# Relational message loop of a four-layer GNN: two pieces share one PSUM bank and one completion signal, sums run twelve pieces behind, sixteen weight slots

## The reference, cut to what matters

```
weight = einsum('rb,bio->rio', w_comp, bases)          # 32 relations, 8 bases
xw     = einsum('ni,rio->nro', h, weight)
msg    = xw[src, rel_type] * norm
out    = segment_sum(msg, dst, num_segments=6250)
x      = layernorm(x + relu(out))
```

## Time and profile before

| | |
|---|---|
| median of three executions | 7899.04 us |
| the profiled execution, device time | 7916.77 us |
| its span, first to last instruction | 7915.0 us |
| granted TensorE clock, mean over the span | 0.803 |
| layer 2's edge loop, first gather to last sum | 3486 to 5045 us |

### The profile page before, as it was taken

How to read it: one execution, slowest core, us unless ns; L and a number is a source line. 1 busy time by engine, 2 the same in 40 slices (tenths; PEclk the granted TensorE clock), 3 DMA queues, 4 the chain that set the end, 5 groups by cost and what they waited for, 6 DMA issues and landing times. The chain is left out here.

```text
span 7915.0 us, 120335 instructions
## 1 busy us (share of the span) xinstructions
PE 5430.0 (69%) x23622; PEld 3980.9 (50%) x23625; DVE 5308.3 (67%) x12633; ACT 2715.6 (34%) x10214; POOL 4371.6 (55%) x7065
## 2 busy tenths in 40 slices
PE   6265666634767676866666666799577777777798
PEld 4133333322444444335555555688455555555687
DVE  8677666676766675546666665774577777777666
ACT  1022222221322222224444444211455555565211
POOL 0377777726777776466666666100466666666311
PEclk8576676666777777877777777999788888888899
DMA  3132333323333333343343333355355555555411
GB/s 109 54 88 81 87 87 87 86 76 105 106 108 107 116 106 91 120 129 113 112 116 110 105 118 108 113 160 162 98 143 143 144 143 140 146 143 140 90 43 38
DMA packets 449612, 865.34 MB, mean 109 GB/s; under 512 B 78488, under 2 KB 284424, under 8 KB 448906
## 3 DMA queue, kind: packets, MB, share of 16 engines
q0 software_dynamic: 194048, 574.45, 26.3%
q1 hardware_dynamic: 238442, 251.25, 10.2%
q10 hardware_dynamic: 16416, 31.99, 1.2%
HBM read 718.55 MB, written 298.46 MB: 128 GB/s over the span
## 5 line engine op out<-in xcount | busy, mean ns | idle before, releaser
L860 PE MATMUL ps<-ring 128*128 x3528 | 1489.4, 547 | 1000.5 <-issue 304.9
L860 PEld LDWEIGHTS ps<-ring 128*128 128x128 f32 x3528 | 727.2, 252 | 1494.2 <-issue 1458.0
L1557 PE MATMUL ps<-big,ring 128*128 128x128 f32 x4928 | 959.8, 355 | 573.6 <-issue 246.6
L834 ACT CAST ring<-ohb 128x128 f32<-128x128 bf16 x1764 | 523.8, 298 | 2044.8 <-DVE ohb L797 1254.8
L1557 PEld LDWEIGHTS ps<-big,ring 128*128 128x128 f32 x4928 | 842.6, 253 | 682.0 <-issue 424.1
L761 POOL DMA_INDIRECT ring<-xl_d,idx x832 | 846.2, 1017 | 611.2 <-DVEq L580 263.5
L1481 POOL DMA_INDIRECT big<-x_d,idx x832 | 805.1, 968 | 572.8 <-ACT ring L1509 425.4
L1773 POOL DMA_INDIRECT ring<-kv_d,gidx x754 | 723.0, 959 | 609.0 <-issue 492.3
L761 POOL DMA_INDIRECT ring<-x_d,idx x832 | 835.3, 1004 | 314.2 <-issue 126.8
L797 DVE TENSOR_SCALAR ohb<-iotab,keyf,nbase 128x128 bf16<-128x128 bf16 x1764 | 588.8, 334 | 463.6 <-remote 174.0
L807 DVE TENSOR_TENSOR big<-big,ps 128x257 f32 (+1 forms) x1764 | 755.0, 428 | 209.8 <-issue 154.9
(11 more groups left out here) (428 smaller groups left out, 9885.8 us busy)
## 6 DMA issues: line engine op xcount, KB each, us to landing
bas_d<-big SPq DMA_DIRECT2D x1232, 128.0 KB
att_d<-wreg SPq DMA_DIRECT2D x464, 132.0 KB
big<-bas_d SPq DMA_DIRECT2D x49, 1024.0 KB, 5.6
x_d<-ring SPq DMA_DIRECT2D x147, 128.0 KB, 1.7
gh_d<-aside ACTq DMA_DIRECT2D x49, 384.0 KB
ring<-xl_d,idx POOLq DMA_INDIRECT x832
ring<-x_d,idx POOLq DMA_INDIRECT x832
big<-x_d,idx POOLq DMA_INDIRECT x832
```

Source lines behind the costliest of these rows:

```text
L834: S.copy(ohf[:, q % G1, :], ohb[:, q % G1, :]).then_inc(e["ohf"], 1)
L860: T.matmul(ps[k][:, 0:D], ohf[:, k, :], rows[:, slot, :].rearrange("p a d -> p (a d)"), start=True, stop=True)
L1557: last = nc.tensor.matmul(ps[c % BANKS2][:, 0:FW].rearrange("p (n h b) -> p n h b", n=NB, h=H)[:, :, h, :], xs[:, j, h * P:(h + 1) * P], w ...
```

## The change

Five things are changed, all in layer 2's edge loop. The weights get 16 slots in place of 8, and VectorE's wait before a group looks 16 pieces back. Two neighbouring pieces write the two halves (256 columns each) of one PSUM bank, so seven banks hold 14 pieces. TensorE signals `l2_mm` after the second piece of a pair, and all waits on `l2_mm` count pairs. It waits for a free bank only before the first piece of a pair. `L2_LAG` goes from 6 to 12. ScalarE's row slots (16), the gather slots (32), the eight running sums and the flush are as before.

```diff
-        wts = nodef[:, 0:8 * P].rearrange("p (s n b) -> p s n b", s=8, b=BASES)
+        wts = nodef[:, 0:16 * P].rearrange("p (s n b) -> p s n b", s=16, b=BASES)
...
                 if past(c, 16):
-                    act.wait_ge(l2_mm, c + GRP - 16)
+                    act.wait_ge(l2_mm, (c + GRP - 16) // 2)
...
-                    if past(c, 8):
-                        dve.wait_ge(l2_mm, c + GRP - 8)
+                    if past(c, 16):
+                        dve.wait_ge(l2_mm, (c + GRP - 16) // 2)
                     for a in range(GRP):
-                        V.scalar_tensor_tensor(out=wts[:, (j + a) % 8], in0=iota[:, 0:NB].unsqueeze(2).broadcast_to([P, NB, BASES]),
+                        V.scalar_tensor_tensor(out=wts[:, j + a], in0=iota[:, 0:NB].unsqueeze(2).broadcast_to([P, NB, BASES]),
...
-                    dve.wait_ge(l2_mm, cc + 1)
+                    dve.wait_ge(l2_mm, cc // 2 + 1)
...
-                                           in1=ps[cc % BANKS2][:, 0:FW], op0=ALU.mult, op1=ALU.add).then_inc(l2_cur, 1)
+                                           in1=ps[cc // 2 % BANKS2][:, cc % 2 * FW:(cc % 2 + 1) * FW], op0=ALU.mult, op1=ALU.add).then_inc(l2_cur, 1)
...
-        L2_LAG = 6
+        L2_LAG = 12
         BANKS2 = 7
...
-                if past(c, BANKS2):
-                    pe.wait_ge(l2_cur, c - BANKS2 + 1)
+                if c % 2 == 0 and past(c, 2 * BANKS2):
+                    pe.wait_ge(l2_cur, c - 2 * BANKS2 + 2)
+                bank = ps[c // 2 % BANKS2][:, c % 2 * FW:(c % 2 + 1) * FW]
                 for h in range(H):
-                    last = nc.tensor.matmul(ps[c % BANKS2][:, 0:FW].rearrange("p (n h b) -> p n h b", n=NB, h=H)[:, :, h, :],
-                                            xs[:, j, h * P:(h + 1) * P], wts[:, j % 8], start=True, stop=True)
-                last.then_inc(l2_mm, 1)
+                    last = nc.tensor.matmul(bank.rearrange("p (n h b) -> p n h b", n=NB, h=H)[:, :, h, :],
+                                            xs[:, j, h * P:(h + 1) * P], wts[:, j], start=True, stop=True)
+                if c % 2:
+                    last.then_inc(l2_mm, 1)
```

## The result

| | before | after |
|---|---|---|
| median, 12 executions each, same chip | 7901.31 us | 7886.35 us |
| ratio | | 0.9981 [0.9972, 0.999] |
| span of the profiled execution | 7915.0 us | 7898.1 us |
| edge loop, first gather to last sum | 1558.7 us | 1544.4 us |

The change takes 15 us off, at 0.19% just what this measurement can tell. Of the 16.9 us between the two profiled spans 14.3 lie in the edge loop; the loop starts 2.2 us earlier, and 0.4 us come behind it.

A forecast was written before the change was run, and what follows sets the result against it. The prediction took SP's flush queue in layer 2's edge loop as the bound. Less SP waiting (33 us) plus an earlier start (5 us) made 38 us off 7899, giving 7861 us, range 7790 to 7920.

The forecast's parts named there:

- the frame: Layer 2's edge loop: SP's flush queue is all but full and sets the pace; VectorE's waits for TensorE are not the bound.
- Rival A: Edge loop: flush queue no bound, VectorE's waits for TensorE are real time; shorter GpSimd gaps give 132 us, 7767 us; chance 0.13.
- Rival C: Edge loop: gathers without gaps leave SP no quick stretch; up to 41 us slower, 7940 us; 0.14 with any other loss.
- rival B: Edge loop: nothing gained, as sums are still signalled late during gathers; within 16 us of 7899; 0.28 with forecast's low end.
- the prediction's sign: Middle of the edge loop: if right, SP's waits for sums fall from 51 us to under 20.
- What VectorE gives SP is an end to SP's own waiting: at most the 51.3 us ... I take three quarters of them, 33 us: Edge loop's middle: VectorE's stock of pieces ends SP's waits for sums; 33 us off, bounds 0 and 51.
- The start, "5 us": Edge loop's start: about four more pieces pass early with the longer lag; 5 us off, bounds 0 and 10.
- The lag: Edge loop: with weight slots, twelve pieces in hand let VectorE work through nearly all of its 5.5 us hole.
- The zeros: Edge loop: one signal for two pieces, ScalarE's wait with GpSimd's gap, and bank halves each change the time by 0.
- The end: Edge loop's last 66 us: twelve sums in place of six follow the last weight; 0, at most 3 us lost.

The follow-up runs named there:

- g0: Kernel before with masked wait values and ScalarE waiting once per group of four pieces, slow instructions (fourth batch): 7928.61 us, 1.0018 against the kernel before.
- g1: Changed kernel with masked wait values and ScalarE waiting once per group of four pieces, slow instructions: 7908.12 us, 0.9995 against the kernel before.
- g2: Changed kernel with the single masked ScalarE wait and sums six pieces behind in place of twelve, slow instructions: 7904.56 us, 0.9995 against the kernel before.
- f0: Kernel before with ScalarE's single masked wait per group, in a batch with quick instructions: 0.9997 against the kernel before (6974.68 us).
- one-wait pair: Kernel before and changed kernel, each with ScalarE's single masked wait per group, slow instructions: 7928.61 us (1.0018) and 7908.12 us (0.9995).
- e5: Changed kernel with masked waits plus one unused semaphore increment per piece on the sync queue: 8022.25 us, 1.0138; masked base 1.0027.
- the fourth batch: Single masked ScalarE wait on the kernel before and the changed one, the latter also with lag six or twelve running sums; unmodified kernel before 7911.71 us.

## Why the prediction was right or wrong

The direction and the frame held. **The bound** is the flush queue: one more instruction costs 87 us, more ring gains nothing, the queue lacked a finished sum for only 28.8 us of 1398 before the change and 4.8 of 1386.5 after it, and VectorE's 410 us of waits turned into 332 us of waits for flushes, as forecast (300 or more). "Remote" fell from 332.8 to 32.5 us, GpSimd's gap stayed near 3.9 us (414.1 us in 104 waits, 3.98 us each), and the loop's 1544.4 us are at the slow end of 1500 to 1545. Rival A, the larger gain, falls with the same rows: TensorE's signals no longer hold VectorE, and a single gap of GpSimd did not shrink; only five of them went, with 11.3 us. Rival C falls too, since the steady part became shorter. The time, 7886.35 us, lies in the range, and in the 16 us around 7899 that rival B gave. B's reason was half right: SP's waits in that view did stay (39.2 of 51.3, where the prediction's sign asked for under 20), but not because sums are signalled late.

**The step that failed is a size: "What VectorE gives SP is an end to SP's own waiting: at most the 51.3 us ... I take three quarters of them, 33 us".** The steady part of the loop became 11.5 us shorter. Two things in the step are wrong, and the records of sums and flushes, compared one by one in the steady part, give both:

```
flush 48 to 1180, us     whole    no finished sum    the rest, SP at work
before                  1398.0     28.8 (70 times)   1369.2
after                   1386.5      4.8 (12)         1381.7
g0 before, one wait     1393.3     54.6 (117)        1338.7
g1 after, one wait      1370.7      7.0 (14)         1363.7
g2 lag 6                1370.6      8.1 (11)         1362.5
f0 quick instructions   1006.9    292.7 (608)         714.2
```

"No finished sum" adds up the times from a flush's issue to the end of the next sum, where that came later. First, the 51.3 us of the waits view were not all hunger: only 28.8 us were. After the change the view still has 39.2 us in 107 waits of 0.37 us, while SP was without a finished sum 12 times and for 4.8 us: such short entries stand for sums that had already ended, and no stock can take them away. Second, of the 24 us of hunger that did go, 12.5 came back as longer work for the same flushes. In the one-wait pair it is 47.6 us and 25.0, the same half. Runs and gaps, split as for e5, show where it came back:

```
flush 48 to 1180      in runs of gathers               in gaps
                      us      flushes  no fin. sum     us      flushes  no fin. sum
before                965.4     577      17.6          432.7     555      11.3
after                 967.6     583       3.4          418.8     549       1.3
```

Without the hunger a flush costs 1.64 us of the queue in a run before the change and 1.65 after it, and 0.76 us in a gap both times. So the 14.2 us of hunger removed in the runs brought six flushes forward, which is worth 6 x 0.76 = 4.6 us of gap, and the 10.0 us removed in the gaps counted in full. That is the counterpart of e5, whose added work came out in the gaps. The one-wait pair moves the same way, with twelve flushes more in the runs (605 and 617), but its flush in a gap costs 0.76 and 0.79 us, so the account is less exact there. Nor does the hunger set the time alone: with one wait of ScalarE the changed kernel has 7.0 us of it, about as much as the 4.8 without, and a steady part 15.8 us shorter. What in ScalarE's instructions does that, no run tells. So the term is the hunger times one half, 12 us, where I had 33; each figure comes from one trace.

**The start, "5 us", was wrong in sign or nothing.** The stall of 30.42 us came apart into stalls of 15.68, 10.25, 6.37 and 4.83 us, but flush 48 is issued 0.8 us earlier after the change, 9.2 us later in the one-wait pair, and 4.7 us later with quick instructions. Sums twelve pieces behind start later (first flush 35.4 in place of 13.0 us), and the queue, which is the bound, stands idle for that time. I counted the pieces that a longer lag lets past, and not those that it holds back.

**The lag was credited with the gain, and has none.** Six and twelve are level at 0.9995. In program order a sum stands behind the next group's weights, so the weights' wait for TensorE, four pieces back, held sums that were ready. Taking that wait away is argued from the traces as the cause (129.6 us of "remote" before weights gone in both, the sums' own of 159.4 left with lag six); it isn't shown apart from the pairs.

**The zeros** were contradicted by nothing, but were tried only under other bounds: a signal for each piece is level with one for two where ScalarE is the bound (1.0021 and 1.0027), and the pairs alone are level with the kernel before where GpSimd is (0.9993). The rule of the Trainium skill, "TensorE: Matmul & The Clock Gate", section "The cost: per-tile semaphore tail", by which 616 increments fewer would be 16 us of TensorE (an estimate), shows nowhere in the time, as hidden work wouldn't. It doesn't show in TensorE's own busy time either (915.0 us with 616 increments more, 921.7 without); the section speaks of the matmuls of several tiles that each increment, and not of increments a piece apart. The end was bounded at 0 to 3 us of loss and taken as 0. From the last gather to the last sum it is 55.6 us before and 59.4 after, 55.1 and 58.0 with one wait, and 22.8 and 25.7 with quick instructions, so the upper bound was about the right value for the way from gather to sum; the flush queue, the bound, made nothing of it (its tail 40.9 and 39.6 us).

The prediction also weighed the rule of the Trainium skill, "DMA: Bandwidth & Descriptors", section "Issuing engines are not separate DMA queues", that the issue is usually small against the DMA. It compares issue with transfer, and no run here shows that, since the profile gives no landing for these flushes. What the runs show is whether the issue matters: with slow instructions a flush costs 1.22 us of the queue in the steady part (1386.5 us for 1132) and the queue is the bound, which the rule would not have led one to expect; with quick ones SP waits for sums for 316.5 us, and it is no bound.

## What to carry to other kernels

When the wait to be removed isn't the bound's own, the gain is at most the time in which the bound has no work, and that is counted from when the work was finished, not from a total of short waits; where the bound's instructions have a dear and a cheap phase, hunger removed from the dear one gives back only part. A longer lag also delays the first delivery to the bound. And before parts of a change are undone one by one, see that the base still has the same waits as the kernel it stands for: one register instruction a copy was enough to move the bound to another engine and to make every part look worthless.

## What the runs showed of the hardware

In layer 2's loop many instructions of SP's and ScalarE's queues take some 0.7 us, single ones 1.4, against 0.03 to 0.24, and mostly while GpSimd issues gathers (527 of SP's 612 over 0.6 us), and signals of TensorE arrive several us late: that is how read. Gathers alone don't do it: in layer 3's loop of the same trace GpSimd issues 928 indirect gathers, and none of the flush's 464 MOVEs takes over 37 ns, none of its DMAs over 343. What layer 2's loop has besides, no run tells. Not expected was that it also depends on the surroundings that the same program meets. In two of five batches, one of them with the chip number of the first, the kernel before took 6975 and 6968 us in place of 7900. With one wait of ScalarE its longest MOVE of the flush was then 42 ns (1424 in the trace of before), a gather still took 974 ns, and the edge loop took 1110 us (1550 in the fourth batch). The granted clock over the loop was 0.94 there and 0.76 in the trace of before. What differs between the two conditions no trace here tells. A kernel tuned in the one may have nothing to gain in the other: there this loop is bound by GpSimd's 1.31 us a gather, and the change takes nothing off it.
